# Transposes of h in the feed-forward phase: three groups of 8, 8 and 6 in three banks, instead of four groups of 6, 6, 5 and 5 in two

## The reference, cut to what matters

```
def _act_quant(x):
    scale = 127.0 / clip(max(abs(x), axis=-1), EPS)
    return clip(round(x * scale), -128.0, 127.0) / scale

gate = silu(bitlinear(x, w_gate))      # 1024 -> 2752
up   = bitlinear(x, w_up)              # 1024 -> 2752
x    = layernorm(x + bitlinear(gate * up, w_down))   # 2752 -> 1024
```

## Time and profile before

| what | value |
|---|---|
| median of 3 runs | 1440.04 us (1439.71 to 1444.51) |
| profiled execution, its own time | 1439.17 us |
| its span | 1437.3 us |
| PE busy | 1373.8 us, 96% of the span |
| DVE busy | 1063.1 us, 74% |
| ACT busy | 616.9 us, 43% |
| POOL busy | 236.7 us, 16% |
| TensorE clock granted over the span | 0.987 of full |

### The profile page before, as it was taken

How to read it: one execution, slowest core, us unless ns; L and a number is a source line. 1 busy time by engine, 2 the same in 40 slices (tenths; PEclk the granted TensorE clock), 3 DMA queues, 4 the chain that set the end, 5 groups by cost and what they waited for, 6 DMA issues and landing times. The chain is left out here.

```text
span 1437.3 us, 23276 instructions
## 1 busy us (share of the span) xinstructions
PE 1373.8 (96%) x7560; PEld 693.6 (48%) x7560; DVE 1063.1 (74%) x1847; ACT 616.9 (43%) x1205; POOL 236.7 (16%) x270
## 2 busy tenths in 40 slices
PE   7878999999999999999999989999999999999996
PEld 3434555455545545554554544444444444444443
DVE  4985565455478677778877768888888888888884
ACT  7666654565455455545545442222222222222221
POOL 0222212213122221222222221000000000000000
PEclk9988999999999999999999999999999999999999
DMA  9505344363534434453443583222222222222200
GB/s 381 206 20 185 133 161 156 127 208 128 174 120 152 162 114 167 145 179 121 142 170 110 138 284 102 74 73 73 73 73 73 73 73 73 73 73 73 75 26 17
DMA packets 63571, 178.92 MB, mean 124 GB/s; under 512 B 15360, under 2 KB 26672, under 8 KB 63536
## 3 DMA queue, kind: packets, MB, share of 16 engines
q1 hardware_dynamic: 63536, 178.48, 38.0%
HBM read 153.02 MB, written 25.43 MB: 124 GB/s over the span
## 5 line engine op out<-in xcount | busy, mean ns | idle before, releaser
L500 PE MATMUL ps<-weights,xT 128*128 128x512 f16 x2112 | 473.6, 381 | 6.4 <-ACT v L753 3.0
L500 PEld LDWEIGHTS ps<-weights,xT 128*128 128x128 f16 x2112 | 204.7, 98 | 244.1 <-issue 14.2
L694 PE MATMUL ps<-weights 128*128 128x512 fp8e4 (+1 forms) x1536 | 300.0, 357 | 0.0
L694 PEld LDWEIGHTS ps<-weights 128*128 128x128 bf16 x1536 | 146.9, 98 | 154.8
L942 ACT ACTIVATE weights<-ps,xscale 128x512 f32<-128x512 f32 x96 | 61.7, 643 | 251.7 <-PE ps L694 251.7
L500 PE MATMUL ps<-weights 128*128 128x512 f16 x768 | 168.6, 379 | 0.4 <-DVE weights L1169 0.4
L722 PE MATMUL ps<-weights 128*128 128x512 fp8e4 x704 | 157.3, 380 | 0.0
L809 ACT ACTIVATE prob<-prob,negmax,undo 128x128 f32<-128x128 f32 x256 | 122.7, 482 | 7.4 <-DVE negmax L1155 7.4
L500 PEld LDWEIGHTS ps<-weights 128*128 128x128 f16 x768 | 75.1, 98 | 90.6 <-DVE weights L1169 0.7
L1492 POOL TENSOR_TENSOR rstd<-rstd,expo 128x1 f32<-128x1 f32 x32 | 17.8, 557 | 535.7 <-DVE rstd L1052 535.7
L722 PEld LDWEIGHTS ps<-weights 128*128 128x128 bf16 x704 | 67.7, 98 | 76.0 <-issue 0.4
(11 more groups left out here) (160 smaller groups left out, 1814.9 us busy)
## 6 DMA issues: line engine op xcount, KB each, us to landing
wch<-w_ffn SPq DMA_DIRECT2D x96, 688.0 KB, 4.3
wch<-sim_scratch SPq DMA_DIRECT2D x96, 128.0 KB
ternary_scratch<-tern SPq DMA_DIRECT2D x48, 172.0 KB, 1.9
ctx<-ctx SPq DMA_DIRECT2D x16, 512.0 KB
wo_raw<-x_scratch SPq DMA_DIRECT2D x16, 512.0 KB, 3.3
out<-k SPq DMA_DIRECT2D x16, 512.0 KB, 2.7
x_in<-xT_in SPq DMA_DIRECT2D x15, 512.0 KB, 6.8
weights<-x SPq DMA_DIRECT2D x15, 512.0 KB, 10.7
```

The lines of the kernel that those rows point to most:

```text
L500: ins = nc.tensor.matmul(ps[:, bank], partsT[:, a, t], weights[:, t, w, half * HALF:(half + 1) * HALF], start=(t == 0 and a + w == 0), sto ...
L694: ins = nc.tensor.matmul(ps[:, 2 * w + a, 0:n], xqT[:, t], w8m[:, t, at:at + n], start=(t == 0), stop=(t == KT - 1))
```

## The change

The 22 transposes are cut into three groups, each with a bank and a pair of semaphores of its own: banks 4, 5 and 3. Bank 3 is one that the gate and up products use, so the transposes also wait for the last odd chunk to be taken out (`pair_free[1]`). A NOP now stands ahead of each group. The down product waits for group 0 before tile 0, for group 1 before tile 8 and for group 2 before tile 16. On DVE there are three evictions in place of four, two ahead of the residual and one behind the norm's sums.

```
-HT_USES = ((0, 6), (6, 12), (12, 17), (17, 22))
+HT_USES = ((0, 8), (8, 16), (16, 22))
...
-        trh_full = [sem("trh_full0"), sem("trh_full1")]
-        trh_free = [sem("trh_free0"), sem("trh_free1")]
+        trh_full = [sem(f"trh_full{u}") for u in range(3)]
+        trh_free = [sem(f"trh_free{u}") for u in range(3)]
...
-        TH, AC = 4, 6
+        TH, AC = (4, 5, 3), 6
...
+                pe.wait_ge(pair_free[1], i * 4 + 4)
                 for u, (lo, hi) in enumerate(HT_USES):
-                    w = u % 2
-                    if not (isinstance(i, int) and i == 0 and u < 2):
-                        pe.wait_ge(trh_free[w], i * 2 + u // 2)
+                    if not (isinstance(i, int) and i == 0):
+                        pe.wait_ge(trh_free[u], i)
                     pe.wait_ge(hq_ready, i * 4 + HQ_NEEDS[u])
-                    bank = ps[:, TH + w].bitcast(BF16)
+                    apart(pe)
+                    bank = ps[:, TH[u]].bitcast(BF16)
...
                 for t in range(IT):
-                    if t in (0, 12):
-                        for w in range(2):
-                            pe.wait_ge(trh_free[w], i * 2 + (1 if t == 0 else 2))
+                    if t in (0, 8, 16):
+                        pe.wait_ge(trh_free[t // 8], i + 1)
                         apart(pe)
...
                 for u, (lo, hi) in enumerate(HT_USES):
-                    w = u % 2
                     if u == 2 and has_next:
                         residual(i + 1, i * 4 + 4)
                         norm_sums(x2n)
-                    dve.wait_ge(trh_full[w], i * 2 + (u // 2 + 1))
-                    src = ps[:, TH + w].bitcast(BF16)[:, 0:(hi - lo) * P].rearrange("p (t n) -> p t n", n=P)
-                    nc.vector.tensor_scalar(hT[:, lo:hi], src, -128.0, None, ALU.max).then_inc(trh_free[w], 1)
+                    dve.wait_ge(trh_full[u], i + 1)
+                    src = ps[:, TH[u]].bitcast(BF16)[:, 0:(hi - lo) * P].rearrange("p (t n) -> p t n", n=P)
+                    nc.vector.tensor_scalar(hT[:, lo:hi], src, -128.0, None, ALU.max).then_inc(trh_free[u], 1)
```

More of the change, by code:

```diff
@@ L702, in turn2 @@
                         pe.wait_ge(pj_free[c], pj_out(B - 1) + 1)
+                pe.wait_ge(pair_free[1], i * 4 + 4)
                 for u, (lo, hi) in enumerate(HT_USES):
-                    w = u % 2
-                    if not (isinstance(i, int) and i == 0 and u < 2):
-                        pe.wait_ge(trh_free[w], i * 2 + u // 2)
+                    if not (isinstance(i, int) and i == 0):
+                        pe.wait_ge(trh_free[u], i)
                     pe.wait_ge(hq_ready, i * 4 + HQ_NEEDS[u])
-                    bank = ps[:, TH + w].bitcast(BF16)
+                    apart(pe)
+                    bank = ps[:, TH[u]].bitcast(BF16)
                     for t in range(lo, hi):
                         ins = nc.tensor.transpose(bank[:, (t - lo) * P:(t - lo + 1) * P], hq[:, t * P:(t + 1) * P], idb[:])
-                    ins.then_inc(trh_full[w], 1)
+                    ins.then_inc(trh_full[u], 1)
                 if not (isinstance(i, int) and i == 0):
```

## The result

The changed kernel takes 1443.09 us (median of 22 runs, 1438.62 to 1447.79) against 1440.09 us before (22 runs, 1435.98 to 1444.51): a ratio of 1.0022, interval 1.0013 to 1.0032. It is slower by about 3 us, clear of no change with this many runs, and under the 0.5% that a few runs can tell. The forecast was 1442.1 us, 2.0 us more than before; the interval of the ratio stands for 1.9 to 4.6 us.

A forecast was written before the change was run, and what follows sets the result against it. PE, busy for 96% of the span, was taken as the bound. +2.2 us over 15 turns and -0.2 us in the last turn gave +2.0 us: 1441.2 us profiled, 1442.1 us as the forecast median, range 1438.0 to 1446.0.

The forecast's parts named there:

- The down product: PE after the transposes of h: waits for the first eviction alone and starts about 0.45 us earlier per turn.
- What is late next: At the x transposes, where PE and DVE arrive together: L1104 comes later, and PE stands still some 0.6 us.
- What DVE has in hand: At the x transposes: L1104's data are ready 0.16 to 0.19 us before PE needs them.
- Sizes of the evictions: DVE ahead of the residual: 1024-element evictions take 0.607 us start to start; two take 1.21 instead of 0.93 us.
- First eviction: DVE behind the first group of eight transposes: starts 0.03 to 0.10 us later, 0.06 taken, NOP included.
- L1057: DVE instruction behind the third eviction: waits for POOL, so at most 0.05 us of the smaller eviction's saving counts.
- The turn: Each turn of phase 2: 0.07 to 0.22 us longer, 0.15 as middle; 15 turns give +2.2 us, 1.0 to 3.3.
- The last turn: Transposes at the slow pace, no next sequence: without the waits between groups they end sooner, -0.2 us.
- Starting the down product earlier buys nothing unless L1104 is earlier too: At the x transposes: claimed an earlier PE alone gains 0, since PE and DVE arrive there together.
- A: Rival, whole turn: PE is the bound throughout and the 0.45 us stay, -7.0 us, 1433.0 us; chance 0.04.
- B: Rival, x transposes: the slip fits into the 0.16 to 0.19 us slack, only 0.2 us go, 1439.8; chance 0.15.
- C: Rival, NOPs ahead of the three groups: breaks cost PE more and DVE waits; +8.7 at 0.6 us, 1448.7; chance 0.07.

The follow-up runs named there:

- e6: Kernel before plus one DVE multiply of 512 float32 elements per partition ahead of the residual, unused by the computation; 35.26 us a turn.
- e7: Kernel after plus one unused DVE multiply of 512 float32 elements per partition ahead of the residual; 35.62 us a turn.
- e5: Kernel before plus one DVE multiply of 128 float32 elements per partition ahead of the residual, unused by the computation; 35.10 us a turn.
- e1: Kernel after without the NOP ahead of each group of transposes; 35.17 us a turn.
- e3: Kernel after with its groups of 8, 8 and 6 in two banks, the third group waiting for the first eviction; 35.27 us a turn.
- e2: Kernel after with the old four groups of 6, 6, 5 and 5, each in its own bank, NOPs kept; 34.94 us a turn.
- e11: Kernel after with the old four groups in four banks and no NOPs; 34.92 us a turn, 1436.95 us, ratio 0.9981 to the kernel before.
- e10: Kernel after, second eviction behind the norm's sums, third behind the scale of x, no NOPs; 34.76 us a turn, 1436.06 us, ratio 0.9975 to the kernel before.
- e4: Kernel after with groups of 6, 8 and 8 in the same three banks, down product waiting at tiles 0, 6 and 14; 35.03 us a turn.
- e8: Kernel after with the second eviction moved behind the norm's sums, beside the third; 34.99 us a turn.

## Why the prediction was right, and where it was off

- *The down product.* Right: it starts 0.44 us sooner, against 0.45 stated.
- *What is late next.* Right: the x transposes, which met L1104 to within 0.2 us before, wait for it in every turn now. e6 makes most of the loss without the change, by a slip on DVE alone, and e7 shows that the slip goes to the turn in full afterwards.
- *What DVE has in hand.* 0.16 to 0.19 us were stated; it is 9.99 - 9.80 = 0.19. e5 fits into it, e6 does not.
- *Sizes of the evictions.* Right: two of 1024 elements start 0.61 us apart (L1091 at 1033.22 less 1032.02, halved: 0.60).
- *First eviction.* The term was mis-sized. It slips by 0.13 us, not 0.03 to 0.10 with 0.06 taken. The NOP costs 0.10 to 0.11 us of it (e1), where I had bounded it at 0.07 by the first weight load of L694, 0.19 us behind L1108. That row bounds nothing: the load of 1042.57 came 0.216 us behind the one ahead of it, at the pace of the matmuls, and not when the NOP let it go. What the NOP costs hangs on where the last release lands. The first group has three waits, and the trace shows them in two instructions, `hq_ready` in one of its own and the other two in the NOP behind it; `hq_ready` is released last, and so the NOP is one more instruction between the release and the load (the wait at 1031.16, the NOP at 1031.27, the load at 1031.34). So `apart` does not hold all the waits ahead of it, as I had it in the section on the kernel before. The third group of e3, whose NOP holds the last release itself, pays 0.02 us. The first eviction's other 0.02 us are the two more transposes, stated at 0.03. The residual slips by 0.40 (0.31 to 0.38 stated).
- *L1057.* Right: it waits 0.20 us for POOL now, and 0.05 us of the slip is lost there. L1104 slips by 0.35 (0.32 taken, 0.26 to 0.38 stated).
- *The turn.* 35.275 us against 35.25 forecast and 35.10 before; 15 turns give 2.6 us, inside the stated 1.0 to 3.3. It is 0.03 us over the forecast, as the slip of L1104 is: the NOP put 0.06 us more on the residual than I took, and of these 0.03 went into the wait for POOL.
- *The last turn.* -0.2 us was forecast. From the fourth quarter of h to the end of the down product it took 12.38 us before and 12.44 after, and to the issue of the final store 17.17 and 17.08. Its down product does start sooner (2.19 instead of 2.40 behind the fourth quarter of h), but more of it runs at half clock. The windows over the slow stretch, after and then before, have 0.50 in the clock column:

```profile
1419.50:1422.90 3.40, 3.40 (x25) 2.63 (x24) 2.38 (x5) 0.00 (x0) 0.00 (x0) 0.50 0.02 5
1422.90:1434.00 11.10, 9.03 (x42) 3.92 (x40) 2.00 (x3) 0.00 (x0) 0.00 (x0) 1.00 0.00 0
```

```profile
1416.80:1420.20 3.40, 3.23 (x24) 2.46 (x25) 2.87 (x7) 0.00 (x0) 0.00 (x0) 0.50 0.02 5
1420.20:1430.00 9.80, 9.33 (x43) 4.02 (x41) 0.52 (x2) 0.00 (x0) 0.00 (x0) 1.00 0.00 0
```

  The clock is back 1420.20 - 1417.15 = 3.05 us behind the fourth quarter of h before, and 1422.90 - 1419.49 = 3.41 after. I had taken the slow pace as given and asked only how long the transposes take at it. The stretch at 0.50 is as long in both, 3.4 us; what differs is where it lies, and that is no effect of the change that the runs show. In each of the thirteen traces PE stands idle for 4.4 to 4.5 us ahead of these transposes and the clock falls, but the place goes from 2.3 us ahead of the fourth quarter (e6) to 0.8 behind it (e5), and the stretch lasts 6.8 us in e2, e6 and e11. The down product then ends between 12.05 us (e7, e10) and 13.53 us (e11) behind that quarter. One trace of each kernel can't show a term of 0.2 us there.
- *The sentence that was wrong.* "Starting the down product earlier buys nothing unless L1104 is earlier too" is false, though the sum beside it was made rightly. It buys the 0.19 us that DVE has in hand: e11, with DVE's work as before, shortens the turn by 0.18 us, and e2, whose NOPs put L1104 back by 0.02, by 0.16. The same error set my expectations for e2 and e4 too high.
- *The rest of the span.* The span grew by 3.3 us and the turns by 2.6. Phase 2 began 0.3 us earlier (the fourth quarter of h in the first turn at 892.0 - 1.36 = 890.64 and 892.1 - 1.76 = 890.34), the last turn gave 0.1 back, and from the issue of the final store, at 1434.32 and 1436.57, to the ends of the spans at 1437.3 and 1440.6 it took 3.0 and 4.0 us. Each of the thirteen traces has about 3.0 or 4.0 us there. The three of the kernel before (e5 and e6 with it) have 3.0, and so have e2, e7 and e11, which are built on the kernel after; what decides it stays open, and with it what the 3.0 us between the medians hold beyond the turns' 2.6.
- *The rivals.* A (PE's gain stays) is refuted for this kernel, but e10 shows what it needed: there L1104 ends 0.35 us earlier than before, and of the 0.55 us by which the down product starts sooner 0.2 are lost at tile 8 and the others reach the turn (0.34). B fell as the slip came to more than the slack. C's place was right, a NOP did cost more than I gave it, but the second group was never late: DVE's two evictions start without a wait between them.

The Trainium skill's page Perfetto Trace Analysis, section Matmul Optimizations, has it that all 8 PSUM banks should be in use. By the traces this holds here only in part: a third bank is worth nothing while the evictions set the pace (e3 against the kernel after, 35.27 and 35.28 us), and a third and fourth are worth 0.16 us a turn where they leave DVE's chain alone (e2). The section Optimizing Scalar/DVE Operations has it that cutting instructions up may let work be done sooner where the Vector engine isn't saturated but keeps others waiting. With this e2 agrees: four evictions in place of three, and banks to match, take 0.34 us off the turn of the kernel after (34.94 against 35.28). Where an instruction stands counts as much: e8 cuts nothing up and only moves one of two evictions behind the residual and the norm's sums, and that is worth 0.28 us a turn.

## What to carry to other kernels

Where a wait is removed, look for the next point at which the same two engines meet, and write down for both when they get there. The engine that comes last sets the time. Bringing it forward gains the smaller of two things: what the edit wins on it, and what the other engine has in hand less whatever the edit adds to that engine's chain. In the kernel after this is 0.19 - 0.35 = -0.16 us, in e2 0.19 - 0.02 = 0.17, and in e10, where the other engine's chain got shorter, it is what PE wins, 0.35; the turns got shorter by -0.18, 0.16 and 0.34. An edit that hands an engine the same work in larger pieces still moves work across the point that another one waits for: count the elements on either side of it, not their sum.

## What the runs showed of the hardware

- A NOP on PE ahead of a weight load costs 0.11 us where the wait that is released last stands in an instruction ahead of it: the first weight load comes 0.22 us behind the end of the second quarter of h with it (1031.34, against 1031.47 - 0.427 + 0.51 - 0.427 = 1031.12, in the kernel after), 0.12 us without it (e1, and the earlier trace rows). Where the NOP itself holds the last release it costs 0.02 us, with PE idle too: 0.07 us from the first eviction's end to the load in e3, 0.05 in the kernel before.
- DVE instructions out of PSUM with bf16 in and out start 0.40, 0.465 and 0.61 us apart at 640, 768 and 1024 elements, their durations being 0.48, 0.55 and 0.69 us: some 0.55 ns an element ((0.61 - 0.40) / 384), and the next one starts about 0.08 us before the end shown.
- The new idle stretch of 0.45 us in each turn left the granted clock at 1.00 over the whole turn, and over all turns from 892 to 1386 us; in e7 it is 0.79 us long, and the clock is 1.00 as well. One turn of the kernel after:

```profile
1031.46:1066.74 35.28, 34.31 (x190) 16.73 (x190) 30.28 (x50) 9.82 (x12) 2.07 (x3) 1.00 0.27 74
```
